# Linear attention in a perceiver block: scores of a 128-token block as one 128x128 product, or as its two diagonal 64x64 quarters in two column tiles

## The reference

```python
hs = layernorm(x)                                   # 512 tokens x 512
q = (hs @ q_w.T + q_b)...; k = ...; v = ...         # 16 heads of 128
qn, kn = l2norm(q / scale), l2norm(k / scale)
gv = softplus(hs @ b_w.T + b_b)[..., None] * v
# chunks of c = 64 tokens
attn = einsum('bnhid,bnhjd->bnhij', qc, kc)         # 64 x 64 a chunk and head
mask = where(j <= i, exp(-0.1 * clip(j - i, 0)), 0)
out = einsum('bnhij,bnhjd->bnhid', attn * mask, gvc)
x = x + (out * silu(hs @ og_w.T)) @ o_w.T + o_b
```

## Time and profile before

| | |
|---|---|
| median of 3 runs | 1001.88 us |
| lowest, highest | 999.18, 1002.01 us |
| span of the profiled execution (first to last instruction) | 1001.3 us |
| instructions | 18374 |
| TensorE matmuls, weight loads | 971.5 us (97%), 838.0 us (84%) |
| VectorE, ScalarE, GpSimd | 69%, 59%, 27% |
| linear attention, rounds 1 to 7 | 409 to 611 us |
| the scores (line 779), all rounds | 15.6 us, 128 matmuls |

### The profile page before, as it was taken

The page is one execution under the profiler, slowest core; times in us unless marked ns, Lnnn a source line. Parts: engine busy times, 40 slices in busy tenths (PEclk is TensorE's granted clock), DMA queues, the critical chain, the costliest instruction groups (busy, mean ns, idle before and its releaser), DMA issues.

```text
span 1001.3 us, 18374 instructions
## 1 busy us (share of the span) xinstructions
PE 971.5 (97%) x5548; PEld 838.0 (84%) x5549; DVE 692.0 (69%) x1053; ACT 593.1 (59%) x966; POOL 271.1 (27%) x170
## 2 busy tenths in 40 slices
PE   9999899999999999999999999989999999999996
PEld 7887798989898987788888888777888888888884
DVE  6655665676567675677876675656677888878886
ACT  6544665666666666445555552541267878778773
POOL 2200230323132142233333310010014545354541
PEclk9999999999999999999999999999999999999999
DMA  9100453321331332222212104410568989998995
GB/s 316 52 1 1 114 185 97 105 83 34 93 105 52 87 96 65 83 84 84 84 63 84 42 21 165 136 43 1 215 224 264 295 269 349 355 347 282 302 354 168
DMA packets 76144, 145.09 MB, mean 145 GB/s; under 512 B 13540, under 2 KB 41060, under 8 KB 75856
## 3 DMA queue, kind: packets, MB, share of 16 engines
q1 hardware_dynamic: 68256, 132.53, 39.2%
q0 software_dynamic: 7856, 12.16, 5.4%
HBM read 146.86 MB, written 15.07 MB: 162 GB/s over the span
## 4 chain that ended last, share of the span: by engine, by line
PE 72%; DMA 8%; SPq 6%; issue 5%; DVE 4%; ACT 4%; DVEq 0%; ACTq 0%; POOLq 0%
PE ps L327 19%; PE ps L328 18%; PE ps L329 18%; PE ps L712 6%; DMA w_and_lists<-in_w 4%; SPq L947 3%; PE ps L980 2%; PE ps L789 1%; DMA y_scratch<-ob,give 1%; PE ps L779 1%; PE ps L769 1%; SPq L1188 1%; DMA w_raw<-in_w 1%; DMA wo_raw<-in_owT 1%; PE ps L992 1%
## 5 line engine op out<-in xcount | busy, mean ns | idle before, releaser
L1005 DVE TENSOR_TENSOR w_l<-w_raw,w_h 128x1408 fp32r<-128x1408 f32 x76 | 121.8, 1624 | 30.9 <-ACT w_h L1001 18.7
L1001 ACT ACTIVATE w_h<-w_raw 128x1408 fp32r (+1 forms) x76 | 103.1, 1376 | 36.6 <-DMA w_raw<-in_w 29.2
L741 POOL TENSOR_TENSOR lw_l<-lw_raw,lw_h 128x1024 fp32r<-128x1024 f32 x32 | 77.1, 2414 | 144.7 <-ACT lw_h L737 139.3
L327 PE MATMUL ps<-w_h,xeT_h 128*128 128x352 f32 x288 | 97.5, 338 | 4.6 <-DVE w_l L1005 4.2
L328 PE MATMUL ps<-w_l,xeT_h 128*128 128x352 f32 x288 | 93.0, 323 | 0.0
L329 PE MATMUL ps<-w_h,xeT_l 128*128 128x352 f32 x288 | 92.9, 323 | 0.0
L1161 POOL DMA_INDIRECT xe<-xn_scratch,take x37 | 39.5, 1069 | 181.6 <-DVE give L1109 100.3
L1165 POOL DMA_INDIRECT y_scratch<-ob,give x34 | 79.7, 2345 | 22.6 <-issue 9.1
L327 PE MATMUL ps<-xT_hi,lw_h 128*128 128x512 f32 x192 | 77.3, 403 | 0.0
L328 PE MATMUL ps<-xT_lo,lw_h 128*128 128x512 f32 x192 | 76.5, 398 | 0.0
L329 PE MATMUL ps<-xT_hi,lw_l 128*128 128x512 f32 x192 | 75.5, 393 | 0.0
(11 more groups left out here) (327 smaller groups left out, 2741.9 us busy)
## 6 DMA issues: line engine op xcount, KB each, us to landing
w_raw<-in_w SPq DMA_DIRECT2D x78, 704.0 KB
w_and_lists<-in_w SPq DMA_DIRECT2D x39, 512.0 KB
w_and_lists<-in_w SPq DMA_DIRECT2D x39, 192.0 KB
rkB<-rk_scratch SPq DMA_DIRECT2D x56, 128.0 KB, 3.1
wq_raw<-in_Wq SPq DMA_DIRECT2D x8, 512.0 KB, 4.5
wo_raw<-in_Wo SPq DMA_DIRECT2D x16, 256.0 KB, 2.9
lw_raw<-in_kwT SPq DMA_DIRECT2D x8, 512.0 KB, 3.3
lw_raw<-in_qwT SPq DMA_DIRECT2D x8, 512.0 KB, 3.4
```

The source lines that it names most:

```text
L327: nc.tensor.matmul(out_ap, lh, rh, start=first, stop=False)
L741: e.tensor_tensor(lw_l[n][:, :, :], lw_raw[n][:, :, :], lw_h[n][:, :, :], ALU.subtract).then_inc(lw_ready[n], 1)
L1001: e.activation(w13_h[:, k, n, :, :], w13_raw[:, slot(raw), n, :, :], ACT.Copy).then_inc(w13_hi_s, 1)
L1005: e.tensor_tensor(w13_l[:, k, n, :, :], w13_raw[:, slot(raw), n, :, :], w13_h[:, k, n, :, :], ALU.subtract).then_inc(w13_ready, 1)
```

## The change

The one product of a head and token tile becomes two, one for each chunk `n` of the tile: weights are the 64 columns of keys of the chunk, moving columns its 64 queries, and the result goes to partitions 0 to 63 (`n = 0`) or 64 to 127 (`n = 1`) of `ps` and to the chunk's 64 columns. A result on partitions 64 to 127 with 64 weight columns is placed in the second of two column tiles of TensorE's array, 128 rows by 64 columns each; one on partitions 0 to 63 in the first. The off-diagonal quarters are not written any more; what stands there is what the keys' projection left in banks 0 and 1, and the mask still multiplies it by zero. Everything else is as before.

```diff
@@ la_pe_at
             e.wait_ge(k_norm, i + 1)
             for k in range(2):
                 for t in range(TT):
-                    tk = slice(t * P, (t + 1) * P)
-                    m = e.matmul(ps[:, k, tk], kq[:, k, tk], kq[:, 2 + k, tk], start=True, stop=True)
+                    for n in range(2):
+                        ch = slice(t * P + n * SQ, t * P + (n + 1) * SQ)
+                        m = e.matmul(ps[n * SQ:(n + 1) * SQ, k, ch], kq[:, k, ch], kq[:, 2 + k, ch],
+                                     start=True, stop=True)
                 m.then_inc(at_ps, 1)
```

## The result

| | before | after |
|---|---|---|
| median of 20 runs each | 1002.37 us | 997.51 us |
| lowest, highest | 999.18, 1007.12 us | 994.44, 1000.63 us |
| ratio, 95% interval | | 0.995 [0.9938, 0.9961] |
| span of the profiled execution | 1001.3 us | 995.1 us |

The forecast was 1004.4 us, slower by 0.2%, in a range from 995.6 to 1010.5. The measured time lies in the range and on its other side: it is the rival "the two tiles work side by side", priced at 998.1. That the range holds it is owed to that rival, which set its lower end, and not to the forecast's own case. In microseconds the interval is a gain of 3.9 to 6.2 (1002.37 x 0.0039 to x 0.0062).

A forecast was written before the change was run, and what follows sets the result against it. TensorE was taken to bound the kernel; unchanged pass time plus 0.35 us a round for the tiles, over seven rounds, added 2.5 us to the 1001.3 us span, plus 0.6 to the median: 1004.4 us, range 995.6 to 1010.5.

The forecast's parts named there:

- the two tiles work side by side: Rival for the scores: both tiles' passes overlap fully, 1.25 us a round instead of 1.79, 3.8 us won; chance 0.27.
- the forecast's own case: Score passes run one behind another, with tile cost: 1004.4 us likeliest, between 1001.9 and 1004.9; chance 0.50.
- What bounds the kernel: TensorE, busy 202.00 of 202.00 us in linear attention rounds 1 to 7; a microsecond there is one of the kernel.
- If the passes come one behind another: Scores: 32 passes a round at 56 ns instead of 16 at 112, 1.79 us either way, no gain or loss.
- the fixed 5 ns: Part of a score pass's 112 ns kept per narrow pass: 58.5 ns each, 0.08 us more a round.
- a load waits for the one ahead: Argument against overlap: in every group, weight loads wait in turn, 112 ns apart with 1 moving column.
- both passes of a product are also on the same tile: Argument against overlap in the scores: a product's two passes follow in a row on one column tile.
- The tile cost: Scores: going into and out of the column tiles loses 0.09 + 0.05 + 0.10 + 0.11 = 0.35 us a round.
- Round 0 counts for nothing: In linear attention round 0 TensorE waits 1.9 us for VectorE's masked scores, so 0.35 us more vanishes there.
- VectorE's spare time covers it: VectorE finishes the first head's masked scores 1.0 us before the products needing them, so later scores make nothing late.
- The slower rival, loads exposed: Narrow score passes pay load and matmul in turn, 111 ns each: 14.8 us lost, 1016.7 us; chance 0.18.
- With neither a loss ... 1001.9: Whole kernel, with no loss going into or out of tiles and no fixed part per pass: 1001.9 us.

The follow-up runs named there:

- two and two: The change with its products reordered: two products of the first tile, two of the second, and so on; 997.99 us, ratio 0.9952.
- four and four: The change with its products reordered: for each head the four products of the first tile, then the four of the second; 999.43 us, ratio 0.9968.
- eight and eight: The change with its products reordered: all eight of the first tile, both heads, then all eight of the second; 1003.14 us, ratio 0.9997.
- the kernel with the heads apart: The change with the second head's scores moved behind the first head's gate projection in rounds 1 to 7, entering the tiles twice a round; 1001.24 us, ratio 0.9992.

## Why the prediction was wrong, point by point

- **What bounds the kernel**: right. TensorE has no gap in rounds 1 to 7 before or after, and 0.57 us off a round came out as 3.96 us of stage.
- **"If the passes come one behind another, 32 x 56 = 1.79 us: nothing is won or lost"**: the step that failed. The price of a pass was right, 58 ns on one tile against 56 (58.5 with the fixed 5 ns, which were assumed). The condition was wrong: on two tiles two passes run in those 58 ns, 0.93 us a round.
- **Why I chose it**: I took "a load waits for the one ahead" and "both passes of a product are also on the same tile" as evidence against overlap. The first holds within one tile; none of the rows had a second. The second is not an obstacle, because TensorE starts a pass of the other tile past as many as three waiting ones: worked out from one order, and met by two others (0.98 and 1.68 us). With rows that could not decide, the chance of 0.27 for the right case was too low, and the Trainium skill's figure for column tiles, cited there, spoke for it.
- **The tile cost, 0.35 us a round**: right, 0.33 to 0.34, measured in the trace and by paying it twice. It takes 2.3 of the 6.2 us that the overlap alone would bring.
- **Round 0 counts for nothing**: right. Its last products start at 406.67 against 406.65; TensorE being earlier only lengthens the wait, to 2.4 us where round 0 ran at the clock's upper level.
- **VectorE's spare time covers it**: right. The masked scores start at 433.92 against 433.94, and no wait came up in rounds 1 to 7.
- **The rival's 998.1 us**: 7 x 0.54 = 3.8 us against 3.96 in the stage. Its median, 997.51, is within what the tail scatters.
- **The slower rival, loads exposed**: out; 58 ns a pass on one tile.
- **"With neither a loss ... 1001.9"**: the reading of the profiled run's place was off. I set the span 0.6 us under the median because the page gave no more; the result lists 996.81 us for the profiled run of the change with its span of 995.1, so a time lies about 1.7 above its span, and the span of before stood for about 1003.0, not 1001.9.

## What to carry to other kernels

Small plain products on two column tiles run at the same time, load and matmul both, if neighbours in the program alternate between the tiles; each visit to the tiles costs about a third of a microsecond here, so gather such products in one place and count visits. The gain needs both the load and the moving columns of a pass halved, or a product whose load is all it has. Ask what the longer version was covering. A wait that grows because TensorE comes to it earlier costs nothing, but work that TensorE now sets off earlier can run into other work: one GpSimd instruction made VectorE 2.4 us late in a single round, and with a stretch at a lower clock behind it that ate the gain of seven.

## What I had not expected of the hardware

The order matters to TensorE across tiles but forgivingly: two and two costs 0.98 us against 0.93, four and four 1.32, eight and eight 1.68 (from the first start to the last). Four tiles of 32 columns take 0.71 us for what two of 64 do in 1.10 and one of 128 in 1.84.

The clock is not at its upper level throughout the profile of the change. In round 0 the change ran 396 to 401 us at 0.70, busy 5.00 of 5.00 us; the profile of the kernel before shows the same stretch at 1.00, with the same kinds of work ahead of it. The change does not bring this: the mean granted clock of single runs is 0.995 to 0.999 with the change and 0.993 to 1.000 for the kernel before, and the two longest times of the change, 1000.05 and 1000.63 us, are the two at 0.995. The kernel with the heads apart, whose round 0 is the change's, had its slow stretch behind the wait instead, where nothing covers it (columns as in the earlier trace rows; the change first):

```profile
396.00:401.00 5.00, 5.00 (x23) 4.18 (x24) 5.00 (x3) 4.34 (x6) 4.42 (x2) 0.70 0.13 44
401.00:406.00 5.00, 4.85 (x47) 3.40 (x45) 4.76 (x9) 0.71 (x2) 2.70 (x2) 0.95 0.71 244
406.00:411.00 5.00, 4.33 (x27) 3.90 (x28) 5.00 (x5) 1.43 (x2) 2.38 (x1) 1.00 0.09 31
```

```profile
401.00:406.00 5.00, 3.08 (x16) 2.17 (x12) 4.77 (x9) 1.66 (x3) 2.79 (x3) 1.00 0.68 232
406.00:411.00 5.00, 4.50 (x21) 4.34 (x22) 5.00 (x5) 0.00 (x0) 2.09 (x1) 0.66 0.40 127
```

In the change it fell where TensorE had slack; in the kernel with the heads apart it is worth some 1.4 us, the 1.8 of round 1 less 0.34. How often it falls where can't be told from one profile a kernel, and it stays open; it is of the size of the spread of the runs.
